# Graph attention over 16 images: the first image's transposes in four banks, its projections in three, its Gram band ahead of the loop, later loads issued later, zero products at the start

## What is computed

```python
alpha = relu(bn(einsum('bchw,oc->bohw', x, wa)))      # queries, 32 channels
sigma = relu(bn(einsum('bchw,oc->bohw', x, ws)))      # keys, 32 channels
att   = softmax(where(spatial_neighbour, alpha^T sigma, NEG))   # 8 neighbours of a pixel
h_s   = einsum('bnm,bcm->bcn', att, x)
Gc    = einsum('bcn,bdn->bcd', x, x)                  # Gram matrix of the channels
catt  = softmax(where(channel_neighbour, Gc, NEG))    # |i - j| == 1
h_p   = einsum('bcd,bdn->bcn', catt, x)
out   = (1 - gama) * x + gama * elu(h_s + h_p)
```

## Time and profile before

| what | value |
|---|---|
| three executions | 478.99, 485.56, 483.58 us; median 483.58 |
| the profiled execution | 483.86 us, of which the recorded span is 482.1 us |
| busy: TensorE, VectorE, ScalarE, GpSimd | 93%, 74%, 70%, 61% of the span |
| mean granted TensorE clock | 0.971 of full speed |

### The profile page before, as it was taken

The page is one execution under the profiler, slowest core; times in us unless marked ns, Lnnn a source line. Parts: engine busy times, 40 slices in busy tenths (PEclk is TensorE's granted clock), DMA queues, the critical chain, the costliest instruction groups (busy, mean ns, idle before and its releaser), DMA issues.

```text
span 482.1 us, 18208 instructions
## 1 busy us (share of the span) xinstructions
PE 450.7 (93%) x7107; PEld 350.2 (73%) x7108; DVE 358.5 (74%) x1139; ACT 339.3 (70%) x980; POOL 295.1 (61%) x198
## 2 busy tenths in 40 slices
PE   1689999899999999999999999999999999999893
PEld 1335777778787786878777786878777787878793
DVE  5006787778877788778878788878778778878866
ACT  2326878587886878678886878777786868778642
POOL 8000376577666766677666766677566756776650
PEclk9997999999999999999999999999999999999856
DMA  6954778677777787778777787777677877533223
GB/s 214 266 142 131 200 221 254 202 239 227 243 235 224 219 254 228 225 235 243 231 236 237 218 256 222 238 236 234 208 247 229 238 224 233 204 133 132 90 88 133
DMA packets 55750, 102.05 MB, mean 212 GB/s; under 512 B 6256, under 2 KB 6640, under 8 KB 55664
## 3 DMA queue, kind: packets, MB, share of 16 engines
q1 hardware_dynamic: 55664, 100.88, 67.9%
HBM read 34.00 MB, written 33.55 MB: 140 GB/s over the span
## 4 chain that ended last, share of the span: by engine, by line
PE 91%; DVE 3%; ACT 2%; issue 2%; DMA 1%; SPq 0%; DVEq 0%; ACTq 0%
PE z L475 34%; PE gb L475 21%; PE xp L485 16%; PE score L475 14%; PE et L560 6%; PE gb L508 1%; ACT upper L253 1%; DMA wt<-w_dram 1%; ACT score L278 1%; DVE z L384 1%; DVE elu L389 0%; DVE score L359 0%; DVE bn L430 0%; ACT L307 0%; DVE probs_t L377 0%
## 5 line engine op out<-in xcount | busy, mean ns | idle before, releaser
L475 PE MATMUL z<-probs_t,upper 64*128 64x128 f32 (+1 forms) x2304 | 175.0, 286 | 5.1 <-DVE probs_t L377 2.1
L475 PEld LDWEIGHTS z<-probs_t,upper 64*128 64x128 f32 x2304 | 157.1, 193 | 24.7 <-issue 21.0
L228 POOL TENSOR_SCALAR elu<-elu,vec,mix 128x1024 f32<-128x1024 f32 x61 | 72.6, 1190 | 160.6 <-DVE elu L389 160.6
L232 POOL TENSOR_TENSOR blend<-elu,blend 128x1024 f32<-128x1024 f32 x61 | 144.2, 2364 | 9.4 <-POOL elu L228 0.5
L302 ACT ACTIVATE elu<-z 128x512 f32<-128x512 f32 x128 | 69.7, 599 | 70.4 <-PE z L475 70.4
L278 ACT ACTIVATE score<-score,neg_max 128x128 f32<-128x128 f32 x256 | 86.6, 338 | 34.8 <-DVE neg_max L359 34.8
L389 DVE SCALAR_TENSOR_TENSOR elu<-elu,z 128x512 f32<-128x512 f32 x128 | 81.9, 681 | 35.2 <-ACT elu L302 35.2
L485 PE MATMUL xp<-const,x 128*128 128x128 f32 x512 | 88.0, 297 | 14.8 <-ACT upper L253 8.8
L384 DVE SCALAR_TENSOR_TENSOR z<-near,catt,z 128x512 f32<-128x512 f32 x128 | 90.2, 749 | 0.8 <-issue 0.4
L485 PEld LDWEIGHTS xp<-const,x 128*128 128x128 f32 x512 | 57.7, 148 | 43.3 <-issue 38.8
L253 ACT ACTIVATE upper<-xp 128x512 f32<-128x512 f32 x128 | 76.9, 600 | 16.3 <-PE xp L485 16.3
(11 more groups left out here) (51 smaller groups left out, 248.7 us busy)
## 6 DMA issues: line engine op xcount, KB each, us to landing
x<-x_dram SPq DMA_DIRECT2D x64, 512.0 KB, 6.0
out_dram<-blend SPq DMA_DIRECT2D x61, 512.0 KB, 3.7
near<-x SPq DMA_DIRECT2D x128, 224.0 KB, 4.5
near<-x SPq DMA_DIRECT2D x128, 30.0 KB, 4.2
out_dram<-blend SPq DMA_DIRECT2D x6, 256.0 KB, 2.0
const<-constants_dram SPq DMA_DIRECT2D x1, 243.5 KB, 9.3
const<-constants_dram SPq DMA_DIRECT2D x1, 128.0 KB, 2.1
wt<-w_dram SPq DMA_DIRECT2D x1, 64.0 KB, 4.1
```

The costliest lines, as they stand in the source:

```text
L228: nc.gpsimd.tensor_scalar(elu[s % 2][:, :, :], elu[s % 2][:, :, :], vec[:, V_GAMA:V_GAMA + 1], mix[:, 1:2], ALU.mult, ALU.add).then_inc(ga ...
L232: nc.gpsimd.tensor_tensor(blend[s % BLENDS][:, :, :], elu[s % 2][:, :, :], blend[s % BLENDS][:, :, :], ALU.add).then_inc(blend_done, 1)
L475: return nc.tensor.matmul(o, l, r, start=start, stop=stop, skip_group_check=True, **kw)
```

## The change

- The transposes of image 0 go into four banks in turn (`xp`, `score`, `et`, `gb`), and a group waits only for the move of the group four before it.
- The projections of image 0 go into three `z` banks and no longer wait for each other's moves.
- `scores(0)` and the whole Gram band of image 0 stand ahead of the first group of transposes of image 1. The z banks are opened between the parts of the band, by zero products without the bf16 identity.
- Twelve products of zeros by zeros (128x512, bf16) stand at the head of TensorE's list, with VectorE's `memset` of the zeros at the head of VectorE's.
- The vectors and weights are loaded through ScalarE's queue, each with a semaphore of its own.
- SyncE's slot -4 waits for the seventh group of transposes (before: the first), slot -3 for `even_done` of image 0 (before: the third group), slot -2 for group 9 (before: 5), slot -1 for group 10 (before: 7), and slot t from 0 on for group 2t + 11 (before: 2t + 9).
- GpSimd zeroes the `near` buffers only after the batch norm, and each `near` buffer is waited for by itself.

```diff
+        def xt_bank(b, q, i):
+            return xp if b else (xp, score, et, gb)[(2 * q + i) % 4]
+        def projections(b):
+            return (gb, gb, gb) if b else (z[0][0], z[0][1], z[1][0])
...
# SyncE
             def build_near(b, q):
                 sp.wait_ge(x_in[b % XBUFS][q], 16 * (b // XBUFS + 1))
+                if b < 2:
+                    sp.wait_ge(near_zero, b + 1)
...
             load_x(0, 0)
-            sp.dma_start(vec[:, :], vectors).then_inc(weights_in, 16)
-            sp.dma_start(wt[:, :, :], w_t).then_inc(weights_in, 16)
...
-            sp.wait_ge(near_zero, 2)
             for t in slots:
                 b, q = t // QUARTERS, t % QUARTERS
-                if b + 1 < B:
-                    sp.wait_ge(xt_done, 2 * t + 2 * QUARTERS + 1)
+                if t == -3:
+                    sp.wait_ge(even_done, 1)
+                elif b + 1 < B:
+                    first = 2 * QUARTERS + (-1 if t == -4 else t + 3 if t < 0 else 2 * t + 3)
+                    sp.wait_ge(xt_done, min(first, 2 * STEPS))
...
# GpSimd
+            pool.wait_ge(bn_done, 1)
             for j in range(2):
                 nc.gpsimd.memset(near[j][:, :, :], 0.0).then_inc(near_zero, 1)
...
# ScalarE
+            act.dma_start(vec[:, :], vectors).then_inc(vec_in, 16)
+            act.dma_start(wt[:, :, :], w_t).then_inc(wt_in, 16)
             act.wait_ge(bn_var, 1)
...
# VectorE
-            dve.wait_ge(ident_in, 16)
-            nc.vector.tensor_copy(ident_b[:, :], ident).then_inc(casts_done, 1)
-            nc.vector.memset(zeros_b[:, :], 0.0).then_inc(casts_done, 1)
-            dve.wait_ge(weights_in, 32)
+            nc.vector.memset(zeros_b[:, :], 0.0).then_inc(zeros_done, 1)
+            dve.wait_ge(vec_in, 16)
...
# TensorE
-                if b + q + i > 0:
-                    pe.wait_ge(xt_out, 2 * QUARTERS * b + 2 * q + i)
+                k, to = 2 * QUARTERS * b + 2 * q + i, xt_bank(b, q, i)
+                if b > 0:
+                    pe.wait_ge(xt_out, k)
+                elif k >= 4:
+                    pe.wait_ge(xt_out, k - 3)
...
+            pe.wait_ge(zeros_done, 1)
+            for _ in range(12):
+                mm(z[1][1][:, :], zeros_b[:, 0:P], zeros_b[:, :], True, True)
             pe.wait_ge(ident_in, 16)
             pe.wait_ge(pads_done, 2 * XBUFS)
-            for t in slots:
+            for q in range(QUARTERS):
+                for i in range(2):
+                    transpose_x(0, q, i)
+            pe.wait_ge(wt_in, 16)
+            project_query(0)
+            project_odd(0)
+            project_even(0)
+            scores(0)
+            for t in range(STEPS + 3):
                 b, q = t // QUARTERS, t % QUARTERS
+                if t == 0:
+                    pe.wait_ge(query_out, 1)
+                    pe.wait_ge(odd_out, 2)
+                    for i in range(2):
+                        gram_band(0, 2 * i)
+                        for h in range(HALF):
+                            last = mm(z[i][h][:, :], zeros_b[:, 0:P], zeros_b[:, :], True, True)
+                        gram_band(0, 2 * i + 1)
+                    last.then_inc(z_open, 1)
                 if b + 1 < B:
                     transpose_x(b + 1, q, 0)
```

More of the change, by code:

```diff
@@ L271, in move_even @@
                 act.wait_ge(even_done, b + 1)
-                nc.scalar.activation(key[b % 2][:, 0:EVEN], gb[:, 0:EVEN], ACT.Relu, bias=bn[:, 7, 1:2],
-                                     scale=bn[:, 6, 1:2]).then_inc(even_out, 1)
+                nc.scalar.activation(key[b % 2][:, 0:EVEN], projections(b)[2][:, 0:EVEN], ACT.Relu,
+                                     bias=bn[:, 7, 1:2], scale=bn[:, 6, 1:2]).then_inc(even_out, 1)
             def exp_scores(s):
@@ L484, in transpose_x @@
                     for h in range(HALF):
-                        last = nc.tensor.transpose(xp[:, v * C + h * P:v * C + (h + 1) * P], xb[:, h, at0:at0 + WIN], ident)
+                        last = nc.tensor.transpose(to[:, v * C + h * P:v * C + (h + 1) * P], xb[:, h, at0:at0 + WIN],
+                                                   ident)
                 last.then_inc(xt_done, 1)
@@ L494, in project_query @@
                     for q in range(QUARTERS):
-                        last = mm(gb[q * HID:(q + 1) * HID, :], wt[:, h, 0:HID], xb[:, h, cols(q)],
+                        last = mm(projections(b)[0][q * HID:(q + 1) * HID, :], wt[:, h, 0:HID], xb[:, h, cols(q)],
                                   h == 0, h == HALF - 1, tile_position=(0, q * HID))
@@ L499, in project_odd @@
             def project_odd(b):
-                xb = xs[b % XBUFS]
-                pe.wait_ge(query_out, b + 1)
+                xb, pj = xs[b % XBUFS], projections(b)[1]
+                if b > 0:
+                    pe.wait_ge(query_out, b + 1)
                 for h in range(HALF):
@@ L504, in project_odd @@
                         odd = xb[:, h, q * QN + 2 * W:(q + 1) * QN + 2 * W].rearrange("p (v m) -> p v m", m=WIN)[:, :, 0:KEYS]
-                        mm(gb[q * HID:(q + 1) * HID, 0:ODD], wt[:, h, HID:], odd,
+                        mm(pj[q * HID:(q + 1) * HID, 0:ODD], wt[:, h, HID:], odd,
                            h == 0, h == HALF - 1, tile_position=(0, q * HID))
                 for h in range(HALF):
-                    last = nc.tensor.transpose(gb[0:KEYS, EDGE + h * P:EDGE + (h + 1) * P],
+                    last = nc.tensor.transpose(pj[0:KEYS, EDGE + h * P:EDGE + (h + 1) * P],
                                                xb[:, h, GROUPS * WIN:GROUPS * WIN + KEYS], ident)
@@ L517, in project_even @@
                         even = xb[:, h, q * QN:(q + 1) * QN + WIN].rearrange("p (v m) -> p v m", m=WIN)[:, :, 0:KEYS]
-                        last = mm(gb[q * HID:(q + 1) * HID, 0:EVEN], wt[:, h, HID:], even,
+                        last = mm(projections(b)[2][q * HID:(q + 1) * HID, 0:EVEN], wt[:, h, HID:], even,
                                   h == 0, h == HALF - 1, tile_position=(0, q * HID))
@@ L581, in z_sums @@
                 last.then_inc(z_done if phase else z_half, 1)
+            pe.wait_ge(zeros_done, 1)
+            for _ in range(12):
+                mm(z[1][1][:, :], zeros_b[:, 0:P], zeros_b[:, :], True, True)
             pe.wait_ge(ident_in, 16)
             pe.wait_ge(pads_done, 2 * XBUFS)
-            for t in slots:
-                b, q = t // QUARTERS, t % QUARTERS
+            for q in range(QUARTERS):
+                for i in range(2):
[5 more added lines that the diff above has]
+            scores(0)
+            for t in range(STEPS + 3):
+                b, q = t // QUARTERS, t % QUARTERS
+                if t == 0:
+                    pe.wait_ge(query_out, 1)
+                    pe.wait_ge(odd_out, 2)
+                    for i in range(2):
+                        gram_band(0, 2 * i)
[3 more added lines that the diff above has]
+                    last.then_inc(z_open, 1)
                 if b + 1 < B:
                     transpose_x(b + 1, q, 0)
-                if t == 0:
-                    pe.wait_ge(casts_done, 2)
-                    for i in range(2):
-                        for h in range(HALF):
-                            last = mm(z[i][h][:, :], ident_b[:, :], zeros_b[:, :], True, True)
-                    last.then_inc(z_open, 1)
-                own = q == 0 and 0 <= b < B
+                own = q == 0 and 0 < b < B
                 if own:
                     gram_band(b, 0)
-                if real(t):
+                if 0 < t < STEPS:
                     scores(t)
@@ L603, in _ @@
                     z_sums(t - 2, 0)
-                if q == 3 and 0 < b + 1 < B:
+                if q == 3 and b + 1 < B:
                     project_even(b + 1)
@@ L613, in _ @@
                     gram_band(b, 3)
-                if q == 2 and 0 < b + 1 < B:
+                if q == 2 and b + 1 < B:
                     project_odd(b + 1)
@@ L617, in _ @@
                     z_sums(t - 2, 1)
-                if q == 1 and 0 < b + 1 < B:
+                if q == 1 and b + 1 < B:
                     project_query(b + 1)
-                if t == -1:
-                    pe.wait_ge(weights_in, 32)
-                    project_query(0)
-                    project_odd(0)
-                    project_even(0)
-                if own:
+                if q == 0 and 0 <= b < B:
                     shift_gram(b)
```

31 lines of the change are left out of this document (17 added, 14 removed).

## The result

| | before | after |
|---|---|---|
| median of four executions each, taken side by side, us | 483.19 (478.99 to 485.56) | 468.63 (468.03 to 469.46) |
| ratio, 95% interval | | 0.9717 (0.9656 to 0.9777) |
| the profiled execution, its span, us | 483.86, 482.1 | 468.35, 466.6 |
| mean granted TensorE clock | 0.971 | 0.974 |

The change saves 14.6 us of the median; the ratio makes it 2.8%.

What follows compares the result with a forecast made beforehand. Steps were taken as bound by TensorE, so only the opening could gain: image 1's query projection 6.5 us earlier, less 0.7 for low clock, gave 5.8; 483.86 - 5.8 = 478.1 us, range 472.5 to 483.5.

Steps and rivals of the forecast that it cites:

- the clock of the opening: TensorE's clock was taken as low (1.2 GHz) until image 0's query projection ends, that projection taking 3.62 us.
- Rival 1: Zero products raise the clock from the transposes on; ninth group ends at 22.8, gain 9.7, 474 us; chance 0.16.
- the same term: Image 0's opening transposes: two groups of 1.10 us each after the fourth quarter's landing, projections starting at 14.6 against 23.20.
- Every later step: SyncE's slots start up to one step, 7.0 us, later; loads and copies have room, so costed at nothing.
- rival 4: Later slots make stores late: GpSimd's keep_x waits, and beyond its slack each of 61 steps grows; 490 us; chance 0.04.
- The tail: End of the kernel: instructions and order as before, no gain counted; shifting low-clock stretches there could move a few us.
- rival 2: Clock stays low after the stall at image 1's query projection, costing 6.75; gain shrinks to 0.9, 483 us; chance 0.13.
- the forecast steps: From ninth group to image 1's projection: slot 3.6 us, landing 6.2, stall 4, projection 3.62 at low clock.
- my 12.0: Time in us when image 0's fourth quarter was expected to land, between estimates of 11.5 and 12.8; before, 13.1.
- the 1.8 of the sum: Two waits for ScalarE between image 0's projections, 26.82 to 27.73 and 29.15 to 30.06, counted as gone: 1.8 us.

Runs made afterwards that it cites:

- one-bank kernel: Changed kernel with image 0's transposes in the one bank xp again, each group waiting for the previous group's move; 480.18 us beside 481.45, ratio 0.9983.
- kernel with tiny products: Changed kernel with the twelve zero products at the head of TensorE's list cut from 512 columns to 1; 471.51 us beside 482.29, ratio 0.9806.

## Why the prediction was wrong

**The step that failed first is the clock of the opening:** "up to the end of that projection the clock is low". It was high from about 5.5 us, during the zero products, until 25.9. Rival 1, which I gave 0.16, came true up to the ninth group, and a little early (21.6 where it said 22.8); its gain of 9.7 at image 1's query projection was measured as 10.6, and behind the low clock there as 9.6. Against it I had held that four groups of 0.59 in the 6 us up to 12 leave TensorE idle over half the time. Eight groups stood there, not four: TensorE was busy for 4.21 us from 6 to 12, behind the zero products. The one-bank kernel shows the case that I had in mind: gaps, and the clock falls at 11.6. Of the two halves of the Trainium skill's rule (TensorE: Matmul & The Clock Gate, "Why this matters for your kernels") the first held in the changed kernel; the second, that idle gaps lose the clock, fits the one-bank kernel, though with gaps of 0.8 us, shorter than those that its row names.

**A second error stood in the same term.** I priced a group of transposes at 1.10, the length of one that stands alone. Back to back at the low clock it takes 0.85. Without any zeros the projections started at 12.74, not at 14.6. So the zeros, on which rival 1 hung, are not even what decides it.

**Every later step: "I cost this at nothing".** 4.2 us came from there in the first pair of traces. The profile before had them in plain sight as 2% of "issue" in the chain, and I asked only what each wait was released by. The experiments show that they return at the same places, that the later release removes half of the places or more, and that a list with other instructions ahead moves them (the kernel without zeros has one of 2.91 us that the kernel with tiny products lacks), as other loads beside the same products did in one trace (1.68 us at 20.34) and not in another. This would fit instructions that arrive late beside data transfers, but no run shows that, and the cause stays open. So does what decides whether the clock falls behind such a pause. The later release, which I counted as a risk alone (rival 4), is itself worth 3 to 4 us of the medians.

**The tail.** From image 15's query projection to the end the four traces of the two lists of before took 56.6, 54.2, 55.6 and 55.5 us, three of the changed kernel 54.9, 56.6 and 55.5. The 1.7 of the first pair are where the clock's low stretches fell, not the change.

**What the first pair flatters.** Image 2's query projection starts at 60.8, 64.0 and 62.2 in three traces of the changed kernel, mean 62.3; in four traces of before with either release at 70.4, 68.9, 68.5 and 68.9, mean 69.2. So the opening is worth 6.9 us on average up to there, though 9.2 up to image 1's query projection (32.1 against 41.2): 2.3 us are given back to a low clock behind the stall, which lasted to 36 us in the first trace and beyond 42 in the second. With rival 2 I had this mechanism: it priced it at 6.75, and the image behind the stall was 1.9, 5.8 and 2.2 us longer than undisturbed in the three traces (1.1 in the first trace of before).

**What held.** The rest of the way to image 1's projection went by the forecast steps: a slot of 3.7 us (3.6), a landing of 6.5 (6.2), a stall of 4.0 (4), a projection of 3.64 (3.62) behind it. The last quarter of image 0 landed at 11.0, before my 12.0 and before the lower bound of 11.5. The two waits between the projections came back with 0.9 each in the kernel with one bank for them: the 1.8 of the sum. No run takes the scores and the band back behind image 1's transposes, so what moving them is worth by itself is not shown. Rival 4's first half came true, and its second not: stores now land after 4.5 us (median of the page; the earlier trace rows had 3.6), GpSimd waits for them for 107.7 us, and the chain by engine has no GpSimd in it: its wait for elu fell from 160.6 to 33.7 us in exchange. With the earlier release given back, stores land after 3.6 us again and GpSimd's wait for them is gone.

## What to carry to other kernels

Where TensorE starts cold behind loads, give its first groups enough banks to stand back to back: that saves the waits, and here it decided the clock of the projections behind them; work out such an opening at both clock levels, from lengths that stand in a row and not alone. A load that is held back by a later point of the list costs its own slot and landing once that point is near the load's reader; count both before trading it for bandwidth that the opening may not need. And read the images one by one: a difference from the undisturbed length shows pauses that no wait explains, and these move with any change to the list or to the time of the transfers.

## What the runs showed of the hardware that was not expected

- TensorE's clock rises during transposes alone: in the kernel without zeros groups took 0.85 us from 7.49 on and 0.44 from 11.87 on, with nothing else on the engine.
- The window's granted clock in the first 10 us of the kernel without zeros (1.00) is no reading: groups of that stretch have the lengths of the low level (0.85, 1.09). The lengths must be read.
- One pause of TensorE of 1.0 us in a steady step was followed by 6.7 us at a clock of 0.51, and the image became 4.3 us longer. In two other executions of the same kernel pauses of 0.5 and 0.7 us at the same place made the image 0.7 and 0.9 us longer. The length alone does not decide it: behind pauses of 0.45 us (opening loads not held back, from 270.4 on) and 0.58 us (kernel before with the later release, from 336.3 on) the clock was 0.50 for over 3 us, and behind one of 0.84 us in the kernel before it stayed at 1.00.
- A VectorE step on 128x2 numbers took 1.60 us beside GpSimd's zeroing and 0.17 with GpSimd idle.
